# Delta attention of a decoder on one core: decays as differences of running sums that a DMA spreads by rows, and the convolution's taps one at a time between DVE's other work

## The chip, the cores and the metric

One core of a Trainium2 chip runs the whole kernel in one launch. The metric is the device time of one execution in microseconds (us). Engines: TensorE (PE), VectorE (DVE), ScalarE (ACT), GpSimd (POOL), SyncE (SP), which here issues all DMAs.

## What is computed

A decoder of four layers works on 32 sequences of 64 tokens with 256 features. Each layer is attention, cross attention and a feed-forward part, each followed by a residual sum and a layer norm. The change touches one part only, the attention of layer 1 (stage a1), a gated delta rule with 16 key heads and 32 value heads of 128 features. Cut to its core:

```
q, k, v = silu(causal_conv4(x @ W_qkv));  z = x @ W_z
beta = sigmoid(b);  g = -exp(A_log) * softplus(a + dt_bias)      # one number a token and value head
q, k = l2norm(q) * DK**-0.5, l2norm(k)
for t:  S = S * exp(g[t]);  S = S + outer(k[t], beta[t] * (v[t] - k[t] @ S));  o[t] = q[t] @ S
y = (rmsnorm(o) * norm_weight * silu(z)) @ W_out
```

The kernel computes the loop over t in closed form for each sequence and head: for tokens i <= t it needs the decay exp(g[i+1] + ... + g[t]), a 64 x 64 triangle, and the inverse of a triangular 64 x 64 matrix.

## The kernel before, in words

Twelve stages follow one another (a0, x0, f0, a1, ... f3), each with a barrier at its ends. Stage a1 is `gated_delta` (L2280 on). It first calls `delta_gates`, which computes g and beta for all tokens and heads; then `load` fetches small constants; then the main block runs.

The work of the main block is cut into 64 blocks: 16 key heads times 4 groups of 512 tokens (8 sequences). A block holds 8 problems (`PROBS`: 4 tiles of 128 tokens times 2 value heads), and on the 128 partitions lie the 64 tokens of two sequences. The order of the work is written by hand, each engine having its own loop over 73 steps k. In step k the block `new` = k is projected, convolved and gets its decays; `turn` = k - 1 gets norms, key products and the triangles N and A; `merge` = k - 8 gets the second half of its inverse and z; `back` = k - 9 is applied to v and summed into `G.x_tok`. Semaphores, waited for by count, tie the engines together.

PE's order in a step: `project` of columns 0 and 1 (L2648, waits for `convolved` of the last step), `mix` (L2658), `norm_sums` (L2670), `key_products` (L2681), `outputs` (L2716), `merge_left` (L2694), `turn_v` (L2727), `merge_right` (L2703), `project` 2 and 3 (waits for the first half of the taps), `sum_squares` (L2737, waits for `x_ready` of `join`), `project_y` first half (L2748), `decay_sums` (L2757), `project_z` (L2769), `project_y` second half (waits for `y_taken` of the first half).

DVE's order: `gates` (L2540), `convolve` of columns 0 and 1 (L2552, six operations), `norms` (L2544, L2545), `scaled_decays` (L2564 to L2575), `gate` (L2587), `attention` (L2580), `join` (L2594), `convolve` of columns 2 and 3, `variance` (L2600, L2601), `add_y` (L2605 to L2612, two halves).

ACT's order: the first tap of columns 0 and 1 (L2448), `keep_m`, `root_norms` (L2457), `keep_yb`, `keep_v` (L2468), `square_o` (L2474), the first tap of columns 2 and 3, `root_o` (L2478), `decay` (the exponential, L2484), `silu_conv` (L2488, L2492), `silu_z` (L2498).

The decays before: DVE multiplies g by the upper triangle `upto`, PE sums that with the triangle `after` into the PSUM tile `kb`, ACT takes the exponential from there. `kb` also takes the key products.

SP issues, step by step, the weights (`fetch_front`, `fetch_back`), the diagonal blocks of N on their way to POOL (`blocks_out`, L2371, L2374) and, every fourth step, the inverses on their way back (`blocks_in`, which waits for POOL and for `mix` of four blocks). POOL inverts 128 blocks of 32 x 32 at a time.

## Time and profile before

| | us |
|---|---|
| runs shown: median of 3 (lowest, highest) | 6177.2 (6168.57, 6228.48) |
| profiled execution, its own time | 6237.58 |
| span of its instructions | 6235.8 |
| PE busy in the span | 5358.3 (86%) |
| DVE busy | 3074.8 (49%) |
| ACT busy | 2093.9 (34%) |
| POOL busy | 788.6 (13%) |
| mean granted clock of PE | 0.879 |

Busy time is the time in which an engine executes; waiting, branching and issuing DMAs do not count. Ends of matmuls are modelled, so PE's busy time is best read from the starts of its groups. The granted clock is the share of TensorE's full clock (2.4 GHz); it is either 1.00 or 0.50 at a time, and a stretch shows the mean.

### The profile page before, as it was taken

To read this page: it belongs to the slowest core of one execution; us is meant where nothing else is said; L and a number is where in the kernel's file an instruction comes from. 1 tells how busy PE (TensorE), PEld (TensorE's weight loads), DVE (VectorE), ACT (ScalarE), POOL (GpSimd) and SP (SyncE) were. 2 spreads that over 40 slices of the span, in tenths; PEclk is the share of its full clock that TensorE was granted. 3 is DMA by queue.
4 is the path that set the end of the run, shared out by engine and by line. 5 is a ranking of instruction groups with operands and counts; after the bars stand their busy time and mean duration, and the time that the engine had idled before them with its cause. 6 is when DMAs were issued, how large, how long until landed. Compare 5 with 4: busy or idle time off the path is not lost. (4 is left out here: it accounts for less than half of the span.)

```text
span 6235.8 us, 85737 instructions
## 1 busy us (share of the span) xinstructions
PE 5358.3 (86%) x34520; PEld 3454.8 (55%) x34520; DVE 3074.8 (49%) x5171; ACT 2093.9 (34%) x2790; POOL 788.6 (13%) x1206
## 2 busy tenths in 40 slices
PE   6339996799999999997977888885699998699798
PEld 4225553466666666665545666663455554344454
DVE  6762223666677676653413565655422226444322
ACT  2211112555555555542223454442111112233211
POOL 2100000332424243240200000000000002000000
PEclk7559997898899899887678999997799998699899
DMA  1114441111111111110100000000244431100143
GB/s 51 22 32 123 126 123 37 35 33 44 29 43 36 33 46 32 42 36 10 30 14 9 13 9 8 13 9 21 71 124 125 123 119 28 42 21 18 25 121 109
DMA packets 373140, 309.34 MB, mean 50 GB/s; under 512 B 235236, under 2 KB 276074, under 8 KB 371616
## 3 DMA queue, kind: packets, MB, share of 16 engines
q1 hardware_dynamic: 372800, 304.59, 17.2%
q8 instruction: 240, 3.93, 0.3%
q14 instruction: 100, 0.82, 0.0%
HBM read 269.76 MB, written 30.11 MB: 48 GB/s over the span
## 5 line engine op out<-in xcount | busy, mean ns | idle before, releaser
L558 DVE TENSOR_TENSOR f_act_g<-f_act_g,f_pu 128x512 f32<-128x512 f32 x288 | 198.1, 688 | 1091.4 <-ACT f_act_g L526 1091.4
L2552 DVE SCALAR_TENSOR_TENSOR a_conv<-a_f,a_cw,a_conv 128x504 f32<-128x504 f32 (+2 forms) x768 | 528.4, 730 | 375.4 <-ACT a_conv L2448 366.3
L526 ACT ACTIVATE f_act_g<-f_pg 128x512 f32<-128x512 f32 x288 | 171.8, 597 | 1365.8 <-PE f_pu L480 1365.7
L2648 PE MATMUL a_f<-g_xT,a_w 128*128 128x512 f32 x1024 | 527.9, 664 | 71.7 <-DVE a_conv L2552 47.3
L497 PE MATMUL f_py<-f_w_out,f_hidden 128*128 128x256 f32 x2304 | 551.0, 382 | 7.0 <-DVE f_hidden L563 7.0
L480 PE MATMUL f_pg<-g_xT,f_w_in 128*128 128x512 f32 x1152 | 548.2, 599 | 0.0
L497 PEld LDWEIGHTS f_py<-f_w_out,f_hidden 128*128 128x128 f32 x2304 | 440.1, 192 | 194.4 <-issue 139.9
L480 PE MATMUL f_pu<-g_xT,f_w_in 128*128 128x512 f32 x1152 | 542.2, 593 | 0.0
L2648 PEld LDWEIGHTS a_f<-g_xT,a_w 128*128 128x128 f32 x1024 | 211.7, 214 | 307.2 <-issue 260.5
L480 PEld LDWEIGHTS f_pu<-g_xT,f_w_in 128*128 128x128 f32 x1152 | 220.0, 191 | 277.0 <-issue 277.0
L2612 DVE SCALAR_TENSOR_TENSOR g_x_tok<-a_b,a_scale,g_x_tok 128x256 f32<-128x256 f32 x512 | 224.3, 480 | 182.4 <-PE a_b L2748 175.9
L480 PEld LDWEIGHTS f_pg<-g_xT,f_w_in 128*128 128x128 f32 x1152 | 220.3, 192 | 162.3 <-issue 147.9
L2426 POOL TENSOR_TENSOR a_Xd<-a_Xd,a_T 128x31 f32<-128x31 f32 (+15 forms) x496 | 282.3, 569 | 38.9
L2748 PE MATMUL a_b<-a_wo,a_og 128*128 128x256 f32 x1024 | 266.2, 406 | 3.4 <-DVE g_x_tok L2612 3.3
L2424 POOL TENSOR_TENSOR a_T<-a_Xd,a_Nd 128x31 f32<-128x31 f32 (+15 forms) x496 | 262.7, 530 | 39.0
L1782 DVE TENSOR_REDUCE x_mx<-x_pX 128x4 f32<-128x1024 f32 x128 | 156.8, 1225 | 211.9 <-PE x_pX L1808 211.9
L1501 POOL MEMSET a_v<- 128x256 f32 x1 | 0.5, 548 | 2041.9 <-POOLq L51 2041.9
L2769 PE MATMUL a_wide<-g_xT,a_wz 128*128 128x512 f32 x512 | 240.0, 612 | 0.0
L2748 PEld LDWEIGHTS a_b<-a_wo,a_og 128*128 128x128 f32 x1024 | 199.5, 202 | 61.1 <-DVE g_x_tok L2612 33.4
L2448 ACT ACTIVATE a_conv<-a_f,a_cw 128x512 f32<-128x512 f32 x256 | 175.3, 685 | 169.9 <-PE a_f L2648 168.7
L2419 POOL MEMSET a_Xd<- 128x1024 f32 x16 | 15.2, 952 | 1679.7 <-DMA a_Nd<-n_blocks 1679.7
L2145 PE MATMUL a_w<-a_w,a_xt 128*128 128x256 f32 x1024 | 226.9, 380 | 0.0
(471 smaller groups left out, 9349.7 us busy)
## 6 DMA issues: line engine op xcount, KB each, us to landing
f_w_in<-in_f_in_w SPq DMA_DIRECT2D x288, 256.0 KB, 3.0
f_w_out<-in_f_out_w SPq DMA_DIRECT2D x288, 128.0 KB, 2.0
f_scale<-f_comb SPq DMA_DIRECT2D x280, 128.0 KB, 3.1
f_scale<-f_comb SPq DMA_DIRECT2D x76, 256.0 KB, 3.4
a_w<-in_a_w SPq DMA_DIRECT2D x16, 512.0 KB, 3.8
n_blocks<-a_N SPq DMA_DIRECT2D x256, 32.0 KB, 1.7
a_Nd<-n_blocks SPq DMA_DIRECT2D x64, 128.0 KB, 2.3
x_blocks<-a_Xd SPq DMA_DIRECT2D x16, 512.0 KB, 3.0
```

Source lines behind the costliest of these rows:

```text
L480: last = pe.matmul(out[:, :], w_in[v][:, 2 * c + k, :], G.xT[:, k, b * BLK:(b + 1) * BLK], start=(k == 0), stop=(k == KC - 1))
L497: last = pe.matmul(py[b % 2][:, t, :], hidden[u][:, t * P:(t + 1) * P], w_out[v][:, :], start=False, stop=False, skip_group_check=True)
L558: dve.tensor_tensor(act_g[u][:, :], act_g[u][:, :], pu[u][:, :], ALU.mult).then_inc(gated, 1)
L2145: last = pe.matmul(out[:, t * 2 * DV:(t + 1) * 2 * DV], xt[:, k, t * P:(t + 1) * P], w[:, k, at:at + 2 * DV], start=(k == 0), stop=(k == K ...
L2424: step(pool.tensor_tensor(t3, Xd[:, 0:left, i:i + 1].to_broadcast([P, left, right]), rows(Nd[kh % 2][:, i, i + 1:HALF], left), ALU.mult))
L2426: last = pool.tensor_tensor(Xd[:, 0:left, i + 1:HALF], Xd[:, 0:left, i + 1:HALF], t3, ALU.subtract)
L2448: act.activation(conv[n % 2][:, j, :], f[j % 2][:, :], ACT.Copy, scale=cw[(n // NBLK) % 2][:, j, TAPS - 1:TAPS]).then_inc(z["tapped"], 1)
L2552: last = dve.scalar_tensor_tensor(out, v3(f[j % 2][:, :], SEQ)[:, :, 0:SEQ - back_by], cw[(n // NBLK) % 2][:, j, TAPS - 1 - back_by:TAPS - ...
L2612: last = dve.scalar_tensor_tensor(y, b2[t % 2][:, h * D:(h + 1) * D], scale[:, 2 * t + h:2 * t + h + 1], y, ALU.mult, ALU.add)
L2648: last = pe.matmul(f[j % 2][:, :], w[u][:, c, j * P:(j + 1) * P], G.xT[:, c, (n % NBLK) * BLK:(n % NBLK + 1) * BLK], start=(c == 0), stop= ...
L2748: last = pe.matmul(b2[t % 2][:, h * D:(h + 1) * D], og[:, h, t * P:(t + 1) * P], wo[(n // NBLK) % 2][:, h, :], start=True, stop=True)
L2769: last = pe.matmul(wide[:, h * BLK:(h + 1) * BLK], wz[u][:, c, h * P:(h + 1) * P], G.xT[:, c, (n % NBLK) * BLK:(n % NBLK + 1) * BLK], star ...
```

## The change

`delta_gates` now goes on after g: PE forms the running sum c of g over the 64 tokens of each sequence (upper triangle `upto`), DVE keeps it as `c_all` with tokens on the partitions, PE turns it, and SP writes it to DRAM and sorts it there by block into `c_rows`, one row of 8 x 64 numbers for each block and sequence half. In the main block SP fetches that row, repeated over 64 partitions, for each half (`fetch_sums`, two buffers `c_row`). DVE's `decays` takes the place of `gates`: it subtracts `c_all` of the block from `c_row` and takes the minimum with 0; ACT takes the exponential of that. `decay_sums` on PE goes, and `key_products` waits for `kq_kept` of the last block instead of `exped`.

DVE's `convolve` is called for one tap (two operations) at a time. The copy of the norms (`take_norms`) stands between the second and third tap of the first two columns, with a semaphore of its own for `merge_left`. `gate` comes ahead of `scaled_decays`. `variance`, then `scales` with the first half of `add_y`, stand between the taps of columns 2 and 3, and the second half of `add_y` behind them. The tiles `conv` lie in `G.y`, which is not used in this stage. PE, ACT and POOL keep their orders otherwise.

```diff
-def delta_gates(nc, G, tag, d, g_all, b_all):
+def delta_gates(nc, G, tag, d, c_all, b_all, c_rows):
...
         w, ba = st.sb("w", [P, KC, 2 * NV]), st.sb("ba", [P, TILES, 2 * NV])
-        dt, a_log = st.sb("dt", [P, NV]), st.sb("a_log", [P, NV])
+        dt, a_log, upto = st.sb("dt", [P, NV]), st.sb("a_log", [P, NV]), st.sb("upto", [P, SEQ])
+        g_all, cT = st.sb("g_all", [P, BLK]), st.sb("cT", [P, TPB, P])
+        by_problem = nc.dram_tensor("c_by_problem", (BLK, 2, SEQ), F32, kind="Internal").ap()
         x, e, u, ln = (st.sb(m, [P, TILES, NV]) for m in ("x", "e", "u", "ln"))
         load(nc, [(w[:, :, :], d["a1_w_ba"]), (dt[:, :], d["a1_dt"].to_broadcast([P, NV])),
-                  (a_log[:, :], d["a1_a_log"].to_broadcast([P, NV]))], st.sem("loaded"))
+                  (a_log[:, :], d["a1_a_log"].to_broadcast([P, NV])), (upto[:, :], d["upto64"])], st.sem("loaded"))
         tile_logits(nc, G, st, w, 2 * NV, ba)
...
-        by_pass = lambda ap: ap[:, :, :].rearrange("p (k b) (t h) -> p (b t) k h", k=16, h=2)
+        g_made, c_made, c_kept, c_turned, ct_kept, c_away, c_sorted = (st.sem(m) for m in (
+            "g_made", "c_made", "c_kept", "c_turned", "ct_kept", "c_away", "c_sorted"))
+        pc, pt = st.ps("pc", [P, BLK]), st.ps("pt", [P, TPB, P])
+        by_pass = lambda ap: ap.rearrange("p (k b) (t h) -> p (b t) k h", k=16, h=2)
         by_head = lambda ap: ap.rearrange("p t (k h) -> p t k h", h=2)
...
                 dve.wait_ge(beta, 1)
-                step(dve.tensor_copy(by_pass(g_all), by_head(x[:, :, :])))
-                step(dve.tensor_copy(by_pass(b_all), by_head(ba[:, :, 0:NV])))
+                dve.tensor_copy(by_pass(g_all[:, :].rearrange("p (n j) -> p n j", j=2 * TPB)), by_head(x[:, :, :])).then_inc(g_made, 1)
+                step(dve.tensor_copy(by_pass(b_all[:, :, :]), by_head(ba[:, :, 0:NV])))
+                dve.wait_ge(c_made, 1)
+                dve.tensor_copy(c_all[:, :, :].rearrange("p n j -> p (n j)"), pc[:, :]).then_inc(c_kept, 1)
+                dve.wait_ge(c_turned, 1)
+                dve.tensor_copy(cT[:, :, :], pt[:, :, :]).then_inc(ct_kept, 1)
+            @block.tensor
+            def _(pe):
+                pe.wait_ge(g_made, 1)
+                for r in (slice(0, SEQ), slice(SEQ, P)):
+                    last = pe.matmul(pc[r, :], upto[r, :], g_all[r, :], start=True, stop=True)
+                last.then_inc(c_made, 1)
+                pe.wait_ge(c_kept, 1)
+                flat = c_all[:, :, :].rearrange("p n j -> p (n j)")
+                for q in range(TPB):
+                    last = pe.transpose(pt[:, q, :], flat[:, q * P:(q + 1) * P], G.ident[:, :])
+                last.then_inc(c_turned, 1)
+            @block.sync
+            def _(sp):
+                sp.wait_ge(ct_kept, 1)
+                for q in range(TPB):
+                    sp.dma_start(by_problem[q * P:(q + 1) * P].rearrange("n s i -> n (s i)"), cT[:, q, :]).then_inc(c_away, 16)
+                sp.wait_ge(c_away, TPB * 16)
+                for r in range(2):
+                    sp.dma_start(c_rows[:, r], by_problem[:, r].rearrange("(n j) i -> n j i", j=2 * TPB)).then_inc(c_sorted, 16)
+                sp.wait_ge(c_sorted, 32)
...
     STEPS = BLOCKS + BACK
-    SLOTS, STATS = 8, 16
+    SLOTS, STATS, NORMS = 8, 16, PROBS
     with Stage(nc, tag) as st:
-        g_all, b_all = st.sb("g_all", [P, BLOCKS, PROBS]), st.sb("b_all", [P, BLOCKS, PROBS])
-        delta_gates(nc, G, tag, d, g_all, b_all)
+        c_all, b_all = st.sb("c_all", [P, BLOCKS, PROBS]), st.sb("b_all", [P, BLOCKS, PROBS])
+        c_rows = nc.dram_tensor("c_rows", (BLOCKS, 2, PROBS, SEQ), F32, kind="Internal").ap()
+        delta_gates(nc, G, tag, d, c_all, b_all, c_rows)
         n_blocks = nc.dram_tensor("n_blocks", (2, P, HALF, HALF), F32, kind="Internal").ap()
...
         gain, one = st.sb("gain", [P, 1]), st.sb("one", [P, 1])
-        upto, after, strict, incl = (st.sb(m, [P, SEQ]) for m in ("upto", "after", "strict", "incl"))
+        strict, incl = st.sb("strict", [P, SEQ]), st.sb("incl", [P, SEQ])
         load(nc, [(gain[:, :], d["a1_gain"]), (one[:, :], d["ones_col"]),
-                  (upto[:, :], d["upto64"]), (after[:, :], d["after64"]), (strict[:, :], d["strict64"]),
+                  (strict[:, :], d["strict64"]),
                   (incl[:, :], d["incl64_scaled"])], st.sem("loaded"))
-        conv = pair("conv", [P, 4, BLK])
+        conv = [G.y[:, u * 8:(u + 1) * 8, :].rearrange("p t e -> p (t e)").rearrange("p (j n) -> p j n", n=BLK) for u in range(2)]
         sq = st.sb("sq", [P, 2, BLK])
-        gt, E = st.sb("gt", [P, PROBS, SEQ]), st.sb("E", [P, PROBS, SEQ])
+        c_row = pair("c_row", [P, PROBS, SEQ])
+        gap, E = st.sb("gap", [P, PROBS, SEQ]), st.sb("E", [P, PROBS, SEQ])
         kk, kq = st.sb("kk", [P, TPB, SEQ]), st.sb("kq", [P, TPB, SEQ])
...
         names = ("w_here0", "w_here1", "cw_here0", "cw_here1", "wz_here0", "wz_here1", "wo_here0", "wo_here1", "wo_scaled",
-                 "projected", "tapped", "convolved", "silued", "squared", "normed", "inverted", "rooted", "kq_made", "kq_kept",
-                 "gt_ready", "decayed", "exped", "n_ready", "a_ready", "v_turned", "v_kept", "nd_away", "nd_here0", "nd_here1", "xd_away", "blocks_turned",
+                 "projected", "tapped", "convolved", "silued", "squared", "normed", "inverted", "norm_taken", "rooted", "kq_made", "kq_kept",
+                 "c_here0", "c_here1", "apart", "decayed", "exped", "n_ready", "a_ready", "v_turned", "v_kept", "nd_away", "nd_here0", "nd_here1", "xd_away", "blocks_turned",
                  "blocks_done", "x_here0", "x_here1", "x_here2", "x_here3", "yb_made", "yb_kept", "x12_made",
...
+                def fetch_sums(n):
+                    if n >= 2:
+                        sp.wait_ge(z["apart"], n - 1)
+                    for s in range(2):
+                        sp.dma_start(c_row[n % 2][half[s], :, :].rearrange("p j i -> p (j i)"),
+                                     c_rows[n, s:s + 1].rearrange("o j i -> o (j i)").to_broadcast([SEQ, PROBS * SEQ])
+                                     ).then_inc(z[f"c_here{n % 2}"], 16)
                 sp.wait_ge(z["set_up"], 1)
+                fetch_sums(0)
                 fetch_front(0)
...
                         fetch_front(k // NBLK + 1)
+                    if is_block(k + 1):
+                        fetch_sums(k + 1)
                     if is_block(k - TURN):
...
                         act.wait_ge(z["a_ready"], n)
-                    act.activation(E[:, :, :], v3(kb[:, :], SEQ), ACT.Exp).then_inc(z["exped"], 1)
+                    act.activation(E[:, :, :], gap[:, :, :], ACT.Exp).then_inc(z["exped"], 1)
...
-                def gates(n):
+                def decays(n):
+                    dve.wait_ge(z[f"c_here{n % 2}"], (n // 2 + 1) * 32)
                     if n:
-                        dve.wait_ge(z["decayed"], n)
-                    dve.tensor_tensor(gt[:, :, :], of_block(g_all, n), rows(upto[:, :], PROBS), ALU.mult).then_inc(z["gt_ready"], 1)
+                        dve.wait_ge(z["exped"], n)
+                    dve.tensor_tensor(gap[:, :, :], c_row[n % 2][:, :, :], of_block(c_all, n), ALU.subtract).then_inc(z["apart"], 1)
+                    dve.wait_ge(z["apart"], n + 1)
+                    dve.tensor_scalar(gap[:, :, :], gap[:, :, :], 0.0, None, ALU.min).then_inc(z["decayed"], 1)
+                def take_norms(n):
+                    dve.wait_ge(z["normed"], n + 1)
+                    dve.tensor_scalar(ss[:, n % STATS, 0, 0:NORMS], eb[:, 0:NORMS], EPS, None, ALU.add).then_inc(z["norm_taken"], 1)
...
                 def norms(n):
-                    dve.wait_ge(z["normed"], n + 1)
-                    step(dve.tensor_scalar(ss[:, n % STATS, 0, :], eb[:, 0:PROBS], EPS, None, ALU.add))
+                    dve.wait_ge(z["norm_taken"], n + 1)
                     dve.reciprocal(ss[:, n % STATS, 1, :], ss[:, n % STATS, 0, :]).then_inc(z["inverted"], 1)
...
-                def convolve(n, pair_):
-                    dve.wait_ge(z["tapped"], n * 4 + 2 * pair_ + 2)
-                    for back_by in range(1, TAPS):
-                        for j in (2 * pair_, 2 * pair_ + 1):
-                            out = v3(conv[n % 2][:, j, :], SEQ)[:, :, back_by:]
-                            last = dve.scalar_tensor_tensor(
-                                out, v3(f[j % 2][:, :], SEQ)[:, :, 0:SEQ - back_by],
-                                cw[(n // NBLK) % 2][:, j, TAPS - 1 - back_by:TAPS - back_by], out, ALU.mult, ALU.add)
-                        if back_by < TAPS - 1:
-                            step(last)
-                    last.then_inc(z["convolved"], 1)
+                def convolve(n, pair_, back_by):
+                    if back_by == 1:
+                        dve.wait_ge(z["tapped"], n * 4 + 2 * pair_ + 2)
+                    for j in (2 * pair_, 2 * pair_ + 1):
+                        out = v3(conv[n % 2][:, j, :], SEQ)[:, :, back_by:]
+                        last = dve.scalar_tensor_tensor(
+                            out, v3(f[j % 2][:, :], SEQ)[:, :, 0:SEQ - back_by],
+                            cw[(n // NBLK) % 2][:, j, TAPS - 1 - back_by:TAPS - back_by], out, ALU.mult, ALU.add)
+                    if back_by < TAPS - 1:
+                        step(last)
+                    else:
+                        last.then_inc(z["convolved"], 1)
...
-                def add_y(n):
+                def scales(n):
                     dve.wait_ge(z["o_rooted"], n + 1)
...
                     step(dve.tensor_tensor(v3(scale[:, :], 2), v3(scale[:, :], 2), cols(rt[:, n % STATS, 1, 0:TPB], 2), ALU.mult))
-                    for two in range(2):
-                        dve.wait_ge(z["y_made"], 2 * n + two + 1)
-                        for h in range(2):
-                            for t in (2 * two, 2 * two + 1):
-                                y = G.x_tok[:, (n % NBLK) * TPB + t, :]
-                                last = dve.scalar_tensor_tensor(y, b2[t % 2][:, h * D:(h + 1) * D], scale[:, 2 * t + h:2 * t + h + 1], y,
-                                                                ALU.mult, ALU.add)
-                            if h == 0:
-                                step(last)
-                        last.then_inc(z["y_taken"], 1)
+                def add_y(n, two):
+                    dve.wait_ge(z["y_made"], 2 * n + two + 1)
+                    for h in range(2):
+                        for t in (2 * two, 2 * two + 1):
+                            y = G.x_tok[:, (n % NBLK) * TPB + t, :]
+                            last = dve.scalar_tensor_tensor(y, b2[t % 2][:, h * D:(h + 1) * D], scale[:, 2 * t + h:2 * t + h + 1], y,
+                                                            ALU.mult, ALU.add)
+                        if h == 0:
+                            step(last)
+                    last.then_inc(z["y_taken"], 1)
...
                     if is_block(new):
-                        gates(new)
-                        convolve(new, 0)
+                        decays(new)
+                        convolve(new, 0, 1)
+                        convolve(new, 0, 2)
+                    if is_block(turn):
+                        take_norms(turn)
+                    if is_block(new):
+                        convolve(new, 0, 3)
                     if is_block(turn):
                         norms(turn)
-                    if is_block(turn):
-                        scaled_decays(turn)
                     if is_block(back):
...
                     if is_block(turn):
+                        scaled_decays(turn)
                         attention(turn)
...
                     if is_block(new):
-                        convolve(new, 1)
+                        convolve(new, 1, 1)
                     if is_block(back):
                         variance(back)
-                        add_y(back)
+                    if is_block(new):
+                        convolve(new, 1, 2)
+                    if is_block(back):
+                        scales(back)
+                        add_y(back, 0)
+                    if is_block(new):
+                        convolve(new, 1, 3)
+                    if is_block(back):
+                        add_y(back, 1)
...
                     pe.wait_ge(z["silued"], n + 1)
-                    pe.wait_ge(z["exped"], n + 1)
+                    if n:
+                        pe.wait_ge(z["kq_kept"], n)
                     b4 = kb[:, :].rearrange("p (w t m) -> p w t m", w=2, m=SEQ)
...
                     if is_block(n + MERGE - TURN):
-                        pe.wait_ge(z["inverted"], n + MERGE - TURN + 1)
+                        pe.wait_ge(z["norm_taken"], n + MERGE - TURN + 1)
                     if n + MERGE >= BACK + 1:
...
                     last.then_inc(z["y_made"], 1)
-                def decay_sums(n):
-                    pe.wait_ge(z["gt_ready"], n + 1)
-                    if n:
-                        pe.wait_ge(z["kq_kept"], n)
-                    for r in half:
-                        last = pe.matmul(kb[r, :], after[r, :], gt[r, :, :], start=True, stop=True)
-                    last.then_inc(z["decayed"], 1)
...
                         project_y(back, 0)
-                    if is_block(new):
-                        decay_sums(new)
                     if is_block(merge):
...
     f = lambda m: m.astype(np.float32)
-    a["upto64"], a["after64"], a["strict64"] = f(r <= c), f(r > c), f(r < c)
+    a["upto64"], a["strict64"] = f(r <= c), f(r < c)
     a["incl64_scaled"] = f(r <= c) * np.float32(P ** -0.5)
...
```

## Rows read from the trace of the kernel before

**Rows 1.** The page, part 1: busy time and share of the span of each engine.
```profile
PE 5358.3 (86%) x34520; PEld 3454.8 (55%) x34520; DVE 3074.8 (49%) x5171; ACT 2093.9 (34%) x2790; POOL 788.6 (13%) x1206
```

**Rows 2.** Windows, PE only: stretch, length, PE busy (instructions), granted clock, DMA share, GB/s.
```profile
1238.30:2717.20 1478.90, 1477.44 (x12314) 0.93 0.15 36
1720.20:2052.70 332.50, 332.47 (x2969) 1.00 0.16 39
1461.60:1491.90 30.30, 30.30 (x233) 0.83 0.05 10
...
1519.80:1533.40 13.60, 13.60 (x121) 0.50 0.29 98
1899.40:1925.00 25.60, 25.60 (x233) 1.00 0.06 12
```

**Rows 3.** Timeline of PE, one step: start us, us, engine line op out<-in, count.
```profile
1899.42 1.95 PE L2670 MATMUL a_eb<-a_one,a_sq 128*128 128x1 f32 x16
...
1910.48 1.84 PE L2737 MATMUL a_eb<-a_one,a_osq 128*128 128x1 f32 x16
...
1914.09 1.08 PE L2757 MATMUL a_kb<-a_gt,a_after 64*64 64x512 f32 x4
1915.09 3.70 PE L2769 MATMUL a_wide<-g_xT,a_wz 128*128 128x512 f32 x8
1918.63 1.89 PE L2748 MATMUL a_b<-a_wo,a_og 128*128 128x256 f32 x8
1920.36 3.60 PE L2648 MATMUL a_f<-g_xT,a_w 128*128 128x512 f32 x8
...
1924.96 1.28 PE L2670 MATMUL a_eb<-a_one,a_sq 128*128 128x1 f32 x10
```

**Rows 4.** Timeline of DVE in the same step; in brackets the idle time before.
```profile
1903.71 0.61 DVE L2564 TENSOR_TENSOR a_bk<-a_b_all,a_ss 128x8 f32<-128x8 f32 x1
...
1906.78 1.28 DVE L2587 TENSOR_TENSOR a_og<-a_b,a_zs 128x512 f32<-128x512 f32 x2
...
1908.75 0.86 DVE L2594 TENSOR_SCALAR a_XT<-a_eb 32x256 f32<-32x256 f32 x2
1911.40 4.20 DVE L2552 SCALAR_TENSOR_TENSOR a_conv<-a_f,a_cw,a_conv 128x504 f32<-128x504 f32 x6 [1.79 <-ACT a_conv L2448]
...
1916.60 1.79 DVE L2612 SCALAR_TENSOR_TENSOR g_x_tok<-a_b,a_scale,g_x_tok 128x256 f32<-128x256 f32 x4
1920.56 1.79 DVE L2612 SCALAR_TENSOR_TENSOR g_x_tok<-a_b,a_scale,g_x_tok 128x256 f32<-128x256 f32 x4 [2.17 <-PE a_b L2748]
1922.27 0.68 DVE L2540 TENSOR_TENSOR a_gt<-a_g_all,a_upto 128x512 f32<-128x512 f32 x1
```

**Rows 5.** Timeline of ACT in the same step.
```profile
1915.91 0.21 ACT L2478 ACTIVATE a_stat<-a_stat 128x8 f32<-128x8 f32 x1 [4.55 <-DVE a_stat L2601]
...
1919.34 1.91 ACT L2488 ACTIVATE a_conv<-a_conv 128x2048 f32<-128x2048 f32 x1
...
1923.15 0.68 ACT L2448 ACTIVATE a_conv<-a_f,a_cw 128x512 f32<-128x512 f32 x1
```

**Rows 6.** Timeline of DVE in delta_gates: a TENSOR_SCALAR from SBUF to SBUF.
```profile
1023.75 0.43 DVE L2250 TENSOR_SCALAR a1g_u<-a1g_e 128x512 f32<-128x512 f32 x1 [0.81 <-ACT a1g_a_log L2268]
```

**Rows 7.** Timeline around the end of delta_gates and the first projection.
```profile
1032.74 0.43 DVE L2262 COPY a_b_all<-a1g_ba 128x512 f32<-128x512 f32 x1
...
1035.26 0.42 SPq L122 DMA_DIRECT2D a_upto<-in_upto  x1
...
1044.95 1.22 PE L2648 MATMUL a_f<-g_xT,a_w 128*128 128x512 f32 x1 [24.48 <-DMA a_w<-in_a_w]
```

**Rows 8.** DMA issues: out<-in engine op xcount, KB each, median us to landing.
```profile
n_blocks<-a_N SPq DMA_DIRECT2D x256, 32.0 KB, 1.7
...
x_blocks<-a_Xd SPq DMA_DIRECT2D x16, 512.0 KB, 3.0
```

**Rows 9.** Timeline of PE in the fill of the pipeline.
```profile
1165.67 6.62 PE L2648 MATMUL a_f<-g_xT,a_w 128*128 128x512 f32 x8 [4.10 <-DVE a_conv L2552]
```

## The prediction

> **What bounds the kernel now.** I read the page first: TensorE (PE) is busy for 86% of the span, DVE for 49% [rows 1]. That is an average over twelve stages, so I went on to the windows of this stage. The change touches only stage a1 (gated delta attention), which runs from about 1002 to 2936 us. Its main loop has 73 steps for 64 blocks. I take the start of L2670, the norm sums, as the mark of a step. The marks of 54 steps lie between 1238.3 and 2717.2 us, 27.4 us apart on average, and in these 1478.9 us PE is idle for 1.5 us [rows 2]. In this stretch the step is as long as PE's own list of work, and what DVE, ACT or a DMA does more or less counts only if PE comes to wait for it.
>
> The timeline of PE in one step at full clock shows the list: 1899.42 to 1924.96, 25.54 us, every group starting where the one before ends [rows 3]. The windows show a second kind of step: 1461.6 to 1491.9 has the same 233 matmuls and takes 30.3 us at a mean granted clock of 0.83 [rows 2]. Others take about 31.9 us. PE is never idle in them, it is at the lower of its levels (1.2 GHz in place of 2.4) for a part of the step. Over the whole stretch the mean granted clock is 0.93, so 7% of 1478.9 us, about 103 us, goes to this. I count 17 such steps of the 54; between 1720.2 and 2052.7 us there is none [rows 2]. It is the largest uncertain sum here, larger than what the change removes.
>
> **What the change removes from PE.** decay_sums goes: two matmuls a block with 64x64 weights and 512 columns, recorded as four. From its start at 1914.09 to the next group at 1915.09 it holds PE for 1.00 us, its busy time being 1.08 us with the overlap [rows 3]. It runs in 64 steps. In the first eight steps PE waits anyway (below), and the last one, in step 63, stands before a wait for ACT. So it counts 55 times: 55 x 1.00 = 55 us off. In steps with a lowered clock these matmuls lie behind the lowered part, so they too are taken at 1.00. Bounds: 50 us, if the steps at both edges of the stretch give nothing, and 60 us at the overlapping 1.08.
>
> **What is late next, on DVE and ACT.** The step becomes 24.54 us if nobody is late. I follow DVE's new order from the mark, in us after it, with durations of rows 4 to 6. Three pairs of taps take 4.20 and so 1.40 each. The first pair of columns is ready at about 0, as before. Taps 1 and 2 end at 2.8, the short copy of the norms (under 0.2) at 3.0, tap 3 at 4.4, the reciprocal at 4.6. gate waits for PE's outputs, which end at 4.9, and takes 1.28: 6.2. The scaled decays, N and A took from 1903.71 to 1908.75 with gate among them, so 3.8 without it [rows 4]: they end at 10.0, where before they ended at 9.3. join (0.86) ends at 10.9, and PE's sum of squares, which waits for it, begins at 11.06 [rows 3]: 0.2 us to spare, the tightest place. (In that step two of these operations were longer than their means, by 0.4 us each; by the means it is 0.9.) The second half of the taps begins at 12.0, behind PE's projection, so its first tap ends at 13.4. variance now comes here, at 13.8 in place of 16.4 [rows 4, 5]. Tap 2 ends at 15.3, the scales at 15.7, the first half of add_y (1.79) at 17.5. PE's second half of project_y waits for that; before it began at 19.21, 0.4 us after DVE had finished the first half [rows 3, 4]. It now wants to begin at 18.21: 0.7 us to spare. With decay_sums removed and DVE in its old order PE would have stood here for some 0.6 us; that is what the new order is worth, and it hides rather than gains. Tap 3 then ends at 19.0, and PE's next projection, which waits for it, begins at 19.94. The second half of add_y waits for PE until 20.1 and ends at 21.9.
>
> decays replaces gates: a subtraction of the size of L2540's product (0.68) and, new, a minimum over 128x512 in SBUF, for which the nearest row is the 0.43 of a TENSOR_SCALAR [rows 4, 6]. Together 1.15 against 0.68, ended at 23.1; DVE then waits for ACT until 24.5 in any case. DVE's work rises by 0.45 us a step, its idle time falls from some 6 to 4.5 us: no cost. The price is from 0 to 0.5 us a step if that cover goes.
>
> On ACT, root_o comes at 13.8 in place of 16.5, and the exponential, which no longer waits for PE, behind it. silu_conv waits for tap 3 at 19.0; before it began at 19.9, held by ACT's own order [rows 5]. It and the two that follow then end at 23.1 and the first tap of the next step begins where PE's columns are ready. That is 1.5 us before the next mark, against 1.8 before: still in time.
>
> **The queue of SP and the DMAs.** Each block now issues two DMAs of 128 KB that spread 2 KB rows over 64 partitions, ahead of the blocks' own DMAs. The issue costs about 0.45 us each [rows 7]. Their wait (`apart` of two blocks ago) is met when SP comes there, and they land a step before DVE reads them. Even behind blocks_in, where SP waits for a mix of PE, there are some 15 us left. The landing of the nearest rows is 1.7 to 3.0 us [rows 8]. I take nothing; lost cover would cost DVE what the landing is late, and PE only beyond 1 us. The move of `conv` into G.y changes no instruction; DVE, ACT and PE read SBUF as before: nothing.
>
> **What it adds: the setup.** delta_gates now goes on behind the copy of b, which ends at 1033.17 [rows 7]. In sequence: the running sums on PE, twice the 1.00 since the clock there is at the lower level, 2.0, begun 0.45 before the copy of b ends; a copy out of PSUM, 0.7; four transposes, for which I take 1.1, between half of that and all of it; a copy, 0.7; four DMAs issued in 1.7 and landed 1.7 later; two more issued in 0.8 and landed 2.5 later [rows 3, 4, 7, 8]; six to seven handovers between engines of some 0.1 to 0.15, 0.8. Sum 11.6 us. Two loads fewer behind it save 0.9, one load more in front costs 0.5, and two issues of fetch_sums ahead of the first weights, which PE waits for [rows 7], cost 0.8: 12 us. Bounds: 8 us if the short DMAs overlap well, 18 us if the sorting DMAs in pieces of 256 B land slowly.
>
> The Trainium skill ("DMA: Bandwidth & Descriptors", Specifications) puts the least transfer for full rate at 512 B; the sorting DMAs lie below it. The row of n_blocks, in pieces of 128 B, lands in 1.7 us [rows 8], so at these sizes the rule moves the setup by less than its bounds.
>
> **The fill.** In the first steps PE waits 4.1 us a step for DVE's last taps [rows 9]; decay_sums stood in front of that wait, so its removal gives nothing. The copy of the norms now stands inside the taps, 0.2 us in seven steps: +1 us. The nine steps behind the last block are unchanged.
>
> **The sum.** -55 + 12 + 1 = -42 us. The profiled execution took 6237.6 us (span 6235.8), so it would take 6195.6. The median of the runs shown is 6177.2, 60 us less, and they scatter over 60 us (6168.6 to 6228.5), of the order of the 103 us that the lowered clock takes. I carry the difference over unchanged: 6135 us, 0.7% less. One per cent is about what a measurement of this kernel can tell from no change.
>
> **The clock.** The clock falls here although PE is never idle: it falls between 1.6 and 3.8 us after the mark (in the step marked 1517.4 it is 0.50 from 1519.8 on, for 13.6 us [rows 2]), while PE works through norm sums, key products and outputs, groups of many short matmuls, and not in each step. Nothing in that part changes, so I take the same loss. The Trainium skill ("TensorE: Matmul & The Clock Gate", section on HAM oscillation) tells one to avoid idle gaps of TensorE to keep the clock; by that rule alone the stretch would have no lowered clock and the change could not move it. The 17 steps contradict it. So a step of 24.5 in place of 25.5 us may meet the falls more or less often, which gives two rivals.
>
> **Rivals.**
> A. The clock falls more often. If the pattern of 1404 to 1715 us, a lowered step every second one, held throughout, 27 steps in place of 17 would lose about 5.8 us each: +58, 6193 us, slower than before. It decides from 8 more such steps. For it: the same pattern stands at 2460 to 2690 us, so it fills over a third of the stretch. Against: the part of the step in which it falls is untouched.
> B. The clock falls less often, as from 1720 to 2052 us. With half the loss gone, -50: 6085 us. By the rows both patterns have some 300 us or more; I give it a little more than A because the runs shown lie mostly below the profiled one.
> C. DVE or ACT becomes the bound: join, tap 3 or add_y's first half comes late, and PE stands every step. It costs once it exceeds 0.5 to 0.9 us of delay; a stall of 0.77 us a step (42/55) eats the gain. A delay of one pair of taps over the slack, 1.4 us, gives 55 x 1.4 = 77, so 6212 us, slower than before. For it: the slack of 0.2 us at join, and two more under 1 us. Against: DVE has 4.5 us idle in the step.
> D. The exchange does nothing because PE's end times are modelled and it in fact waited for DVE. Then only the setup remains: 6190 us. Against: all groups start back to back in 54 steps.
>
> **How the numbers follow.** Forecast 0.55, A 0.13, B 0.20, C 0.08, D 0.04. Under 6115 us (faster by over 1%) lie B and a quarter of the forecast's scatter: 0.20 + 0.14 = 0.34. Over 6239 us lie only the far ends of A and C: 0.06. Within 1%: 0.60. The range takes in A and most of B: 6060 to 6200 us.
>
> **What would show it.** Right: no matmul on kb besides key products; steps at full clock of 24.5 us with PE idle under 1%; PE's second project_y begins at 18.2 with DVE's first add_y ended before; the minimum takes 0.43 us; first projection 12 us later. Wrong: waits of PE for g_x_tok, a_XT or a_conv inside the stretch, or a mean granted clock there away from 0.93 by over 0.02, which is 30 us.

## The result, and the profile after

The changed kernel takes 6276.6 us (median of 4 runs, 6261.8 to 6327.3) beside 6178.8 us before: 1.0143 times as long, 95% interval 1.0092 to 1.0194. The forecast was 6135 us, 0.7% faster, with a range of 6060 to 6200 us. What it said of work and waits came out nearly; what it said of the clock did not.

In this section and below, a step is taken from one start of norm_sums to the next, "lowered" are steps in which TensorE stands at 1.2 GHz for a part, "lost" is what a stretch takes beyond its steps at full clock, and the 54 steady steps are the same ones as in [rows 2]. Windows of PE over them, in the changed kernel: stretch, length, PE busy (instructions), granted clock, DMA share, GB/s; below the whole stretch a part with full clock and a part without.

```profile
1249.50:2740.00 1490.50, 1489.66 (x12099) 0.87 0.18 45
1512.00:1585.00 73.00, 73.00 (x676) 1.00 0.24 63
1711.70:1803.90 92.20, 92.20 (x677) 0.78 0.19 50
```

The second row holds three steps in 73 us, the third three steps with the same work in 92.2 us. The whole stretch is 12 us longer than before, although its list of work is shorter: the mean granted clock went from 0.93 in [rows 2] to 0.87. PE is idle for 0.8 us in it.

The timeline of PE in a step at full clock answers to [rows 3]:

```profile
1512.00 1.95 PE L2734 MATMUL a_eb<-a_one,a_sq 128*128 128x1 f32 x16
...
1523.06 1.84 PE L2802 MATMUL a_eb<-a_one,a_osq 128*128 128x1 f32 x16
1524.77 1.97 PE L2813 MATMUL a_b<-a_wo,a_og 128*128 128x256 f32 x8
1526.58 3.60 PE L2826 MATMUL a_wide<-g_xT,a_wz 128*128 128x512 f32 x8
1530.01 1.89 PE L2813 MATMUL a_b<-a_wo,a_og 128*128 128x256 f32 x8
1531.74 3.60 PE L2712 MATMUL a_f<-g_xT,a_w 128*128 128x512 f32 x8
1535.26 1.15 PE L2722 MATMUL a_wide<-a_A,a_XT 64*64 64x64 f32 x32
1536.34 0.83 PE L2734 MATMUL a_eb<-a_one,a_sq 128*128 128x1 f32 x6
```

From 1512.00 to 1536.34 are 24.34 us, 1.2 less than before. project_z follows the first half of project_y at once. No matmul of this step waits: DVE and ACT are in time.

DVE in the same step, answering to [rows 4 and 6]:

```profile
1521.06 0.86 DVE L2645 TENSOR_SCALAR a_XT<-a_eb 32x256 f32<-32x256 f32 x2
1523.98 1.39 DVE L2602 SCALAR_TENSOR_TENSOR g_y<-a_f,a_cw,g_y 128x504 f32<-128x504 f32 x2 [2.07 <-ACT g_y L2492]
...
1527.53 1.79 DVE L2664 SCALAR_TENSOR_TENSOR g_x_tok<-a_b,a_scale,g_x_tok 128x256 f32<-128x256 f32 x4
1529.24 1.35 DVE L2602 SCALAR_TENSOR_TENSOR g_y<-a_f,a_cw,g_y 128x488 f32<-128x488 f32 x2
...
1531.94 1.79 DVE L2664 SCALAR_TENSOR_TENSOR g_x_tok<-a_b,a_scale,g_x_tok 128x256 f32<-128x256 f32 x4 [1.35 <-PE a_b L2813]
1533.64 0.68 DVE L2585 TENSOR_TENSOR a_gap<-a_c_row,a_c_all 128x512 f32<-128x512 f32 x1
1534.36 0.43 DVE L2587 TENSOR_SCALAR a_gap<-a_gap 128x512 f32<-128x512 f32 x1
```

join ends at 1521.92, 1.1 us before the sum of squares; the first half of add_y ends at 1529.32, 0.7 us before the second half of project_y; the last tap ends at 1530.59, 1.15 us before the next projection. The subtraction takes 0.68 us and the minimum 0.43.

Where the clock falls shows in PE's timeline of a lowered step, and in windows of three parts of it:

```profile
1333.92 1.95 PE L2734 MATMUL a_eb<-a_one,a_sq 128*128 128x1 f32 x16
1335.80 1.82 PE L2746 MATMUL a_kb<-g_y 128*64 128x128 f32 x16
1337.55 3.68 PE L2781 MATMUL a_b<-a_M,a_V 64*128 64x64 f32 x32
1341.16 1.92 PE L2759 MATMUL a_eb<-a_XT,a_N 32*64 32x32 f32 x32
1343.00 1.97 PE L2792 MATMUL a_wide<-g_ident,g_y 128*128 128x128 f32 x8
...
1345.90 5.55 PE L2712 MATMUL a_f<-g_xT,a_w 128*128 128x512 f32 x8
```

```profile
1333.90:1336.00 2.10, 2.10 (x24) 1.00 0.15 23
1336.00:1349.60 13.60, 13.60 (x125) 0.50 0.36 81
1349.60:1364.60 15.00, 15.00 (x86) 1.00 0.08 27
```

PE has been busy without a gap, and 2.1 us after the start of norm_sums it goes to the lower level for 13.6 us. outputs takes 3.6 us from start to start in place of 1.9. The next step begins at 1364.56, 30.6 us after this one, and it falls at the same place again: seven of the steady steps from 1274 to 1487 us are lowered one after the other. In all, 30 of the 54 are lowered, against 17 in the profile before.

Of the 30 falls, 29 come 2.0 to 3.9 us after the start of norm_sums, and 27 of these have no idle time of PE above 0.05 us in the 25 us before them. The remaining one is of another kind: it comes 14.6 us after the mark, lasts 3.4 us, and follows sum_squares, the step's other group of one-column matmuls, in front of which PE had waited 0.2 us for join.

The account between the two profiled executions:

| | before | after | difference, us |
|---|---|---|---|
| start of the first norm_sums | 1071.1 | 1085.2 | +14.1 |
| from there to the steady steps | 167.2 | 164.3 | -2.9 |
| 54 steady steps, at full clock (25.55, 24.34 each) | 1379.5 | 1314.6 | -64.9 |
| 54 steady steps, lost (98 and 174 of it in lowered steps) | 99.4 | 175.9 | +76.5 |
| behind the steady steps | 3518.6 | 3526.9 | +8.3 |
| span | 6235.8 | 6266.9 | +31.1 |

That is 31 us, and the medians differ by 98: the profiled execution of before was one of its longer ones; the first experiment shows by what. Of the 8.3 us behind the steady steps, 4.9 are the very next step, which is lowered further in the changed kernel (30.4 us against 25.5, granted clock 0.76 against 0.98).

### The profile page after: what moved, and what is told of

Read it like the earlier page. It is cut to its first block and busy times, and to the rows that moved or that the text cites. A ratio compares the mean times of both kernels' runs of the same rounds, so it can differ in the third digit from the quotient of the medians.

```text
span 6266.9 us, 85624 instructions
## 1 busy us (share of the span) xinstructions
PE 5369.2 (86%) x34272; PEld 3511.5 (56%) x34272; DVE 3107.9 (50%) x5237; ACT 2096.9 (33%) x2790; POOL 792.8 (13%) x1206
## 5 line engine op out<-in xcount | busy, mean ns | idle before, releaser
L2602 DVE SCALAR_TENSOR_TENSOR g_y<-a_f,a_cw,g_y 128x504 f32<-128x504 f32 (+2 forms) x768 | 526.7, 728 | 347.9 <-ACT g_y L2492 344.9
L2712 PE MATMUL a_f<-g_xT,a_w 128*128 128x512 f32 x1024 | 556.8, 694 | 77.9 <-DVE g_y L2602 57.0
L2492 ACT ACTIVATE g_y<-a_f,a_cw 128x512 f32<-128x512 f32 x256 | 174.8, 686 | 220.1 <-PE a_f L2712 219.1
```

Source lines behind the costliest of these rows:

```text
L2492: act.activation(conv[n % 2][:, j, :], f[j % 2][:, :], ACT.Copy, scale=cw[(n // NBLK) % 2][:, j, TAPS - 1:TAPS]).then_inc(z["tapped"], 1)
L2602: last = dve.scalar_tensor_tensor(out, v3(f[j % 2][:, :], SEQ)[:, :, 0:SEQ - back_by], cw[(n // NBLK) % 2][:, j, TAPS - 1 - back_by:TAPS - ...
L2712: last = pe.matmul(f[j % 2][:, :], w[u][:, c, j * P:(j + 1) * P], G.xT[:, c, (n % NBLK) * BLK:(n % NBLK + 1) * BLK], start=(c == 0), stop= ...
```

## The experiments

The theory: the change does what was forecast to the work, and loses it through the lower clock, which meets a step of 24.3 us more often; the fall needs norm_sums standing among other short matmuls. The rivals: DVE's new order costs time, or the spreading DMAs and the minimum do, or the other stages do. "PE windows" is the same view as above for the 54 steady steps. In the runs that were timed together with each group the kernel before had a median of 6196 to 6198 us, 18 us higher than in the first comparison; ratios are to those, and differences between kernels are of their medians. The changed kernel was timed in the first comparison only; taken from the ratios, the distances to it below come out 5 to 12 us larger. Every kernel but the one before has one profile, so its count of lowered steps is that of one execution.

**The kernel before, again.** No edit.

> The kernel before, unchanged, for a second profile and more times. The first theory (the clock theory: the change lengthens the stage because TensorE stands at 1.2 GHz for a part of more steps) says that executions of this kernel differ by how many steps have a lowered clock: a profiled execution near 6177 us should show a mean granted clock of about 0.96 to 0.97 in the 54 steady steps of stage a1, against 0.93 in the profile of 6237 us. A rival (other stages make the spread between executions) says 0.93 again and the difference elsewhere.

6190.7 us, ratio 1.0005 (0.9976 to 1.0033). The profiled execution has a span of 6181.6 us, 54 us less than the one shown before. PE windows:

```profile
1238.80:2667.70 1428.90, 1428.85 (x12314) 0.96 0.16 38
```

The steady steps take 50.0 us less than in [rows 2], with the same number of matmuls, and the clock is 0.96: 8 lowered steps, 49 us lost. 50 of the 54 us between two executions of one kernel lie here. Beside this execution the changed kernel's profile is 85 us longer, made up of 126.5 more lost in the steady steps, 64.9 less work in them, 14 more up to the first norm_sums, 3 less from there to the steady steps and 13 more behind them.

**The matmuls put back.**

```diff
+                def refill(n):
+                    if n:
+                        pe.wait_ge(z["kq_kept"], n)
+                    for r in half:
+                        pe.matmul(kb[r, :], incl[r, :], G.xT[r, 0, 0:BLK], start=True, stop=True)
...
                         project_y(back, 0)
+                    if is_block(new):
+                        refill(new)
```

> The changed kernel with two matmuls of the size of decay_sums put back at their old place (64x64 weights, 512 columns, into kb; nothing reads the result, so the output is unchanged). Clock theory: the full-clock step goes from 24.3 back to 25.5 us, fewer steps have a lowered clock, and in spite of 1.2 us more work in each of 64 steps the time falls, from about 6276 to about 6195 us (the kernel before plus the 14 us of setup). Rival (DVE's new order, the DMAs or the minimum cost the time): the time stays or rises by up to 66 us, to 6276 to 6340 us.

6209.9 us, ratio 1.0026 (0.9998 to 1.0053). With 1.2 us more work in each step the kernel is faster by 67 us than the changed one. The step at full clock is 25.55 us again and 15 steps are lowered:

```profile
1251.10:2716.20 1465.10, 1463.90 (x12314) 0.94 0.18 46
```

Everything of the change but the absence of two matmuls is in this kernel. What remains over the kernel before, 12 us, is of the size of its setup (the first norm_sums begins at 1086.5 against 1071.6), though by the interval it is not clear of nothing. The steady step is as long as before, so with these matmuls in place neither DVE's order, the DMAs nor the minimum cost it anything.

**A wide matmul inside the run of short ones.**

```diff
                         norm_sums(turn)
+                        fill(turn)
                         key_products(turn)
...
+                def fill(n):
+                    if n:
+                        pe.wait_ge(z["kq_kept"], n)
+                    pe.matmul(kb[:, :], G.ident[:, :], G.xT[:, 0, 0:BLK], start=True, stop=True)
```

> The changed kernel with one more matmul of 128x128 weights and 512 columns (about 0.86 us at full clock) between norm_sums and key_products; its result is overwritten, the output is unchanged. It splits the run of short matmuls in which the clock was seen to fall. Clock theory in its stronger form (the fall needs that run of short matmuls behind the mark): hardly any steady step has a lowered clock, mean granted clock over 0.97, step 25.2 us, time about 6276 - 185 + 55 = 6145 us. Weaker form (only the length of the step matters): a step of 25.2 us, some lowered steps as in the kernel before, 6180 to 6260 us. Rival without the clock: 6276 + 55 = 6330 us.

6186.6 us, ratio 0.9979 (0.9960 to 0.9999): 90 us faster than the changed kernel with about 1.0 us more work a step. The time lies in the range of the weaker form (only the length of the step counts), near its fast end; the stronger form asked for 6145 us and hardly any lowered step, and it missed.

```profile
1248.80:2675.60 1426.80, 1424.98 (x12207) 0.96 0.18 47
```

The step at full clock is 25.31 us and 60 us are lost, in 17 steps, 12 of which lose only 1.6 to 3.8 us. One wide matmul behind norm_sums shortens most of the lowered parts but does not do away with them, and since it also lengthens the step, this run does not tell the effect of the place from that of the length.

**DVE's order alone.** The kernel before with the DVE half of the diff: one tap at a time, take_norms, gate ahead of scaled_decays, variance, scales and add_y between the taps; gates and decay_sums stay.

> The kernel before with DVE's new order alone: one tap at a time, the copy of the norms, gate, variance, scales and add_y between, while decays stay with gates and decay_sums on TensorE. Clock theory: step still 25.5 us, TensorE without idle time, clock as in the kernel before: 6178 us within 1%. Rival (the new order costs time): slower by over 1%, up to 6276 us.

6198.2 us, ratio 0.9984 (0.9956 to 1.0012). 25.55 us a step, 13 lowered. The order costs nothing and gains nothing that could be measured while decay_sums is there.

**The sums left out, old order.** This kernel leaves out the summing of the decays over tokens: the exponential is taken of the product of gates.

```diff
-                    act.activation(E[:, :, :], v3(kb[:, :], SEQ), ACT.Exp).then_inc(z["exped"], 1)
+                    act.activation(E[:, :, :], gt[:, :, :], ACT.Exp).then_inc(z["exped"], 1)
...
-                    if is_block(new):
-                        decay_sums(new)
```

> The kernel before with decay_sums left out: ACT takes the exponential of the product of gates directly, so the decays are not summed over tokens; DVE's order is the old one, and there is no setup, no spreading DMA and no minimum. Clock theory: the full-clock step is 24.3 us plus a wait of TensorE for the first half of add_y of some 0.6 us, so about 24.9 us, and the number of lowered steps is what decides the time; with a step of 24.9 us I expect a count between that of before (8 to 17) and of the changed kernel (30): 6150 to 6240 us. Rival (less work on TensorE is less time): 6198 - 35 to 6198 - 65, so 6133 to 6163 us.

6216.8 us, ratio 1.0040 (1.0012 to 1.0068). The step at full clock is 25.46 us, 0.1 less than with decay_sums in it; 24.9 was expected. The waits of PE over the steady steps say why (who waited for whom, us in total, times, longest):

```profile
PE a_b L2749 <- DVE g_x_tok L2612: 48.9, 54, 1.3
```

In each step the second half of project_y stands for DVE's first half of add_y, 0.9 us of idle time, and the weight loads stand longer. Removing the matmuls in the old order moves the time from work to a wait. The step length is nearly the old one and so is the count of lowered steps, 11. So the absence of the two matmuls does not bring the lowered steps by itself, and an idle gap of 0.9 us in each step does not either.

**The sums left out, new order.** The same omission on the kernel with DVE's new order.

> The same omission with DVE's new order, still without setup, spreading DMA and minimum. Clock theory: the step at full clock is 24.3 us without waits, some 30 of 54 steady steps are lowered and take 29 to 30.7 us, mean granted clock 0.86 to 0.89, and the time is that of the changed kernel less its setup of 14 us and the same after the loop: 6250 to 6270 us. Rival (the DMAs, the minimum or the larger traffic bring the lowered steps): clock 0.93 or more and 6120 to 6160 us.

6323.7 us, ratio 1.0206 (1.0167 to 1.0246). 24.34 us a step at full clock and 41 of 54 lowered:

```profile
1237.90:2807.00 1569.10, 1568.77 (x12100) 0.82 0.14 34
```

There is no setup, no spreading DMA and no minimum in this kernel, and it is the slowest of all. The loss comes with the step of 24.3 us. The time is some 55 us over the range expected: the count of lowered steps was not to be foretold, 30, 36 and 41 in three kernels whose steps have the same length.

**norm_sums ahead of the projections.** The changed kernel with norm_sums moved; no work is added or left out. ACT and DVE are rearranged so that the squares and norms are in time.

```diff
                 for k in range(STEPS):
...
+                    if is_block(turn):
+                        norm_sums(turn)
                     if is_block(new):
                         project(new, 0)
                         project(new, 1)
...
-                        norm_sums(turn)
                         key_products(turn)
...
-                    act.activation(conv[n % 2][:, :, :], conv[n % 2][:, :, :], ACT.Silu).then_inc(z["silued"], 1)
+                    act.activation(conv[n % 2][:, 0:2, :], conv[n % 2][:, 0:2, :], ACT.Silu).then_inc(z["qk_silued"], 1)
...
                     act.activation(sq[:, :, :], conv[n % 2][:, 0:2, :], ACT.Square).then_inc(z["squared"], 1)
+                    act.wait_ge(z["convolved"], 2 * n + 2)
+                    act.activation(conv[n % 2][:, 2:4, :], conv[n % 2][:, 2:4, :], ACT.Silu).then_inc(z["silued"], 1)
```

> The changed kernel with norm_sums moved ahead of the first projection of the step (between the second half of project_y and project), with no work added on TensorE. To have the squares in time ACT takes silu of q and k first, then the squares, then silu of v; DVE takes the norms and scales E ahead of the taps. Clock theory in its stronger form (the clock falls in the run mix, norm sums, key products, outputs because norm sums lie in it): few lowered steps, step 24.3 us, 6110 to 6150 us. Weaker form (only the step's length counts): as the changed kernel, 6276 us. If the new order makes TensorE wait: waits of TensorE for a_sq or g_y in the trace and a longer full-clock step.

6126.0 us, ratio 0.9892 (0.9854 to 0.9930), 151 us faster than the changed kernel. PE windows:

```profile
1283.30:2601.60 1318.30, 1316.36 (x12096) 1.00 0.20 51
```

Two lowered steps of 54. The cost is in the fill: from the first norm_sums to the steady steps it takes 205 us in place of 164. The waits of PE in that stretch:

```profile
PE a_eb L2739 <- ACT a_sq L2536: 49.4, 8, 6.2
PE a_f L2717 <- DVE g_y L2604: 22.0, 8, 3.0
```

There PE has nothing else to do while it waits for the squares, and the projections stand behind norm_sums. The 8.5 us lost in the steady steps are not all the clock's: the two lowered steps take 4.4 of them.

**norm_sums between the two projections.**

```diff
                     if is_block(new):
                         project(new, 0)
+                    if is_block(turn):
+                        norm_sums(turn)
+                    if is_block(new):
                         project(new, 1)
```

> As the kernel with norm_sums moved, but between the two projections, so that matmuls of 512 columns stand on both sides of the norm sums. Stronger form: the fewest lowered steps of all, 24.3 us a step, 6100 to 6140 us, at or below the kernel with norm_sums ahead of both projections. Weaker form: 6276 us. A wait of TensorE would show in front of key products or the sums of squares.

6088.2 us (6083.9 to 6090.5), ratio 0.9829 (0.9791 to 0.9866): the fastest kernel, 1.7% under the kernel before and 188 us under the changed one. PE windows, and its timeline around the moved group:

```profile
1254.60:2572.90 1318.30, 1316.13 (x12098) 1.00 0.20 51
```

```profile
1912.70 1.89 PE L2819 MATMUL a_b<-a_wo,a_og 128*128 128x256 f32 x8
1914.43 1.88 PE L2718 MATMUL a_f<-g_xT,a_w 128*128 128x512 f32 x4
1916.14 1.84 PE L2740 MATMUL a_eb<-a_one,a_sq 128*128 128x1 f32 x16
1917.85 1.96 PE L2718 MATMUL a_f<-g_xT,a_w 128*128 128x512 f32 x4
1919.74 1.15 PE L2728 MATMUL a_wide<-a_A,a_XT 64*64 64x64 f32 x32
```

The same matmuls, back to back as before, in another order, and the clock stays. The time is 12 us under the range expected. Two lowered steps remain, 4.6 us of the 8.5 lost, and neither falls at the old place: both come about 2.3 us after the start of sum_squares, in front of which PE had waited for DVE's join (0.16 and 0.62 us), and last 3.4 us. One of them, in PE's timeline and in its window:

```profile
1782.32 1.92 PE L2808 MATMUL a_eb<-a_one,a_osq 128*128 128x1 f32 x16 [0.62 <-DVE a_XT L2651]
1784.60:1788.00 3.40, 3.40 (x8) 0.50 0.39 143
```

The four runs of this kernel lie within 7 us; the 13 of the kernel before beside them scatter over 55 us. The fill takes 170 us, near the old 164.

**norm_sums between the projections, decay_sums kept.** The last kernel's order on the kernel before: gates and decay_sums stay, and there is no setup and no spreading DMA.

> The kernel before (gates and decay_sums kept, no setup, no spreading DMA) with DVE's new order and norm_sums moved between the two projections, as in the fastest kernel so far. Clock theory: hardly any lowered step here either, full-clock step 25.5 us, so 54 x 1.2 = 65 us more than that kernel in the steady steps and 14 us less setup: 6088 + 51 = 6139 us. That would be the worth of the change with the clock held: about 50 us. If it is not over 6115 us, the exchange of the decays is worth nothing by itself; if it is near 6197 us, the clock's gain needs the shorter step.

6132.5 us, ratio 0.9899 (0.9871 to 0.9927). PE windows:

```profile
1250.00:2624.70 1374.70, 1374.70 (x12313) 1.00 0.16 39
```

No lowered step, 25.46 us each. Beside the kernel above it differs by the exchange of the decays alone, and is 44 us slower. That is the worth of the exchange with the clock nearly held. By the profiles, 42.6 us apart, it is 65 us less work and 8.5 more lost in the steady steps, 16 more up to the first norm_sums, 11.5 less from there to the steady steps, and 9 more behind them. Beside the kernel before, this one shows that moving norm_sums (with the order of DVE and ACT that goes with it) is worth 64 us without the change, more than the change itself.

**silu split alone.** The changed kernel with ACT's part of the edit above, norm_sums at its old place.

> The changed kernel with ACT's silu split alone (silu of q and k, squares, silu of v), norm_sums at its old place. A control for the two kernels that move norm_sums. Clock theory: no effect on TensorE's order, so 24.3 us and about 30 lowered steps, 6250 to 6290 us. Rival (the split of silu gave the gain): 6090 to 6130 us.

6279.4 us, ratio 1.0125 (1.0092 to 1.0158). 36 lowered steps:

```profile
1249.20:2785.50 1536.30, 1536.16 (x12101) 0.84 0.17 44
```

The split of silu gives nothing. What DVE's part of the rearrangement (the norms and the scaling of E ahead of the taps) does at the old place was not run alone; PE's list is the same and it hardly waits in any of these kernels, so the gain is put down to the place of norm_sums; that much is argued.

All kernels side by side, sorted by place of norm_sums and length of the step at full clock:

| kernel | step at full clock, us | lowered of 54 | lost, us | ratio |
|---|---|---|---|---|
| sums out, new order | 24.34 | 41 | 254.5 | 1.0206 |
| silu split alone | 24.34 | 36 | 221.7 | 1.0125 |
| the change | 24.34 | 30 | 175.9 | 1.0143 |
| wide matmul behind norm_sums | 25.31 | 17 | 60.0 | 0.9979 |
| sums out, old order | 25.46 | 11 | 67.8 | 1.0040 |
| before (two profiles) | 25.55 | 17, 8 | 99.4, 49.4 | 1, 1.0005 |
| matmuls put back | 25.55 | 15 | 85.6 | 1.0026 |
| order alone | 25.55 | 13 | 73.0 | 0.9984 |
| norm_sums ahead of projections | 24.26 | 2 | 8.5 | 0.9892 |
| norm_sums between projections | 24.25 | 2 | 8.5 | 0.9829 |
| the same, decay_sums kept | 25.46 | 0 | 0.0 | 0.9899 |

In the two rows with 8.5, about half (4.4 and 4.6 us) is lost in the lowered steps.

## Why the prediction was wrong

**The bound: right.** The steady step is PE's list of work, in all kernels but the one that leaves the sums out in the old order.

**decay_sums, 55 us: right in kind, a little small.** The step shrank by 1.21 us, not by 1.00. The start of the group to the start of the next missed what stood around it: project_y's first half holds PE 1.81 us where it held 1.91, and project_z 3.43 where it held 3.54. 54 steps give 65 us.

**DVE's new order: right, its worth too small.** It was called worth 0.6 us a step, hiding rather than gaining. Alone it does nothing; without it PE stands 0.9 us a step and the removal gains 0.1 us. Part of that was a misreading: [rows 3] and [rows 4] put the start of project_y's second half 0.24 us behind DVE's first half (1918.63 against 1918.39), not 0.4, and the wait is then 0.8 us. The slacks were forecast as 0.2 (join), 0.7 and 0.9 and are 1.1, 0.7 and 1.15 us in the step shown; join's was read from a step in which two of DVE's operations were stretched. Rival C did not happen.

**The minimum, SP's queue, the DMAs: right.** 0.43 us as the row said. The spreading DMAs land in 3.1 us (median), and DVE waited for them once, ahead of its first block. Their issue takes 0.60 us each (median) where 0.45 was reckoned, which only the setup felt (1.12 us for two, 0.8 reckoned). With the two matmuls put back, the steady step is 25.55 us as before.

**The setup, 12 us: right.** The first projection begins 13.3 us later (1058.22 against 1044.95), the first norm_sums 14.1. Its parts in the timeline:

```profile
1033.42 1.97 PE L2277 MATMUL a1g_pc<-a1g_g_all,a1g_upto 64*64 64x512 f32 x4 [12.28 <-DVE a1g_g_all L2266]
...
1038.13 1.75 SPq L2289 DMA_DIRECT2D c_by_problem<-a1g_cT  x4
1041.09 1.24 SPq L2292 DMA_DIRECT2D c_rows<-c_by_problem  x2
1046.72 0.34 SPq L122 DMA_DIRECT2D a_gain<-in_a_gain  x1
```

From the first of these matmuls to the first DMA are 4.7 us, where the four operations were reckoned at 4.5 without handovers. The two sorting DMAs took 1.24 us to issue where 0.8 was reckoned, and landed in 2.8 for 2.5.

**The clock: the step that failed.** The text took the loss of 103 us over unchanged, because "nothing in that part changes" where the clock falls. The part did not change, and the loss still went from 49 to 99 us up to 176. What was missed is that the number of falls in it goes with the length of the step: at 25.5 us, falls come mostly in every second step and for long stretches not at all; at 24.3 us a lowered step takes 30.6 us and the next one often falls at the same place. The text's own sign of being wrong, a mean granted clock over 0.02 away from 0.93, shows it: 0.87. Rival A named this, as one lowered step in two and +58 us, with a chance of 0.13; the truth was over one in two against one in three to seven, and the result lies 84 us above A's 6193.

The sum of the rest, -42 us, is close to what the change is worth with the clock nearly held: 44 us (6132.5 less 6088.2). Part of this fit is luck. The profiles of those two kernels differ by -56.5 us in the steady steps (65 of work less 8.5 lost), where -55 was forecast; by +16 up to the first norm_sums and -11.5 from there to the steady steps, for +12 and +1; and by +9 behind them, for nothing. The misses cancel.

**The median and the profiled execution: a second, smaller slip.** The text knew that the executions of before scatter over 60 us, "of the order" of the clock's loss, and still used the profiled one's loss of 99 us as the typical one. The second profile lost 49. From the typical execution the rise to the new loss is 126 us, from the profiled one 77. The range went 65 us over the forecast, half of that 126.

What stays open is what exactly makes the clock fall. Shown is: it falls while PE is busy without a gap; with norm_sums in its old place, 185 of the 191 falls in nine profiles come in the run of norm sums, key products and outputs, 1.6 to 3.9 us after the mark. The other six, and three of the four in the kernels with norm_sums moved, come 1.9 to 3.2 us after the start of sum_squares, the other group of one-column matmuls, when PE had waited 0.13 to 0.62 us for join just before it; each lasts 3.4 us. Shown too is that only none or two of 54 steps are lowered when norm_sums stands beside a projection, with the same matmuls; and with norm_sums in its old place the three kernels with a step of 24.3 us lose 176 to 255 us, those with 25.3 to 25.55 us 49 to 99 us.

That the length itself does it is argued, not shown: each of the longer steps also holds decay_sums, a matmul in its place or a wait of 0.9 us, and no run changed the length by other means. The loss follows neither from a short step alone (24.25 us with norm_sums moved loses almost nothing) nor from the matmuls' absence alone. Why 30, 36 or 41 steps are lowered at the same length was not tried.

## What to carry to other kernels

Where TensorE is busy without a gap and its mean granted clock is still below 1.00, the lost time is a term of its own, and it can outweigh the work that a change removes: find the group during which the clock falls, and if it holds one-column matmuls, try them between wide ones before shortening anything. Here that worked for one group; whether other short matmuls behave alike was not tried. A loop that meets such a group once a step can lose more when its step gets shorter; so compare a change at a held clock, or profile several executions of both kernels. And when a removal is planned, look who comes to wait: here the removal alone was worth 0.1 us a step and the order of another engine turned it into 1.2.

## What was not expected of the hardware

The lower level came with PE idle for 0.8 us in 1490. The Trainium skill ("TensorE: Matmul & The Clock Gate", section on HAM oscillation) gives idle gaps as what to avoid. In these traces most falls need no gap, and moving norm_sums, eight matmuls of one column recorded as sixteen, to another place in the same list brings the mean granted clock from 0.87 to 1.00. The instructions of norm_sums count as busy in the profile, 1.95 us of each step. And a gap of 0.9 us in each step, as with the sums left out in the old order, went with 11 lowered steps, no more than in the kernel before.

The scatter between executions goes with the clock: the kernel before took 6155.99 to 6236.92 us in 31 runs, and its mean granted clock over the whole execution was 0.893 in the first of these and 0.879 in the last. Two of the kernels with a steady clock of 1.00 scatter by 7 and 8 us in four runs each, the third, with decay_sums kept, by 24.
